# Idle-time products of a constant in the first stage of a fused state-space and channel-mix kernel

## What is computed

```python
mod = (silu(c) @ wmod).reshape(4, 6, 1, 512)
sa, ca, ga, sb, cb, gb = ...           # ga, gb pushed away from 0 to at least 0.25
h = layernorm(x) * (1 + ca) + sa
omega = clip(softplus(h @ W_omega.T + b_omega), 1e-4, 100); zeta = sigmoid(h @ W_zeta.T + b_zeta)
A = omega**2; S = 1 / (1 + 1e-4 * A); d = 1 - zeta; F = h @ W_B.T + b_B
# step: z' = d*(S*z - 0.01*A*S*y) + F_z ;  y' = d*(0.01*S*z + S*y) + F_y
x = x + ga * (states @ C.T + h @ D_mat.T)
h = layernorm(x) * (1 + cb) + sb
xr = mu_r*h + (1-mu_r)*h_prev;  xk = mu_k*h + (1-mu_k)*h_prev
x = x + gb * (sigmoid(xr @ W_r.T) * (relu(xk @ W_k.T)**2 @ W_v.T))
```

## Time and profile before

| | |
|---|---|
| median of three runs | 959.48 us (959.30 to 960.77) |
| the profiled execution | 959.10 us, of which the span is 957.3 us |
| TensorE busy | 932.2 us, 97% of the span |
| VectorE, ScalarE, GpSimd busy | 86%, 73%, 10% |
| mean granted clock of TensorE | 0.989 |
| the chain that ended last | 85% PE, 6% DVE, 6% ACT, 2% DMA |

### The profile page before, as it was taken

The page is one execution under the profiler, slowest core; times in us unless marked ns, Lnnn a source line. Parts: engine busy times, 40 slices in busy tenths (PEclk is TensorE's granted clock), DMA queues, the critical chain, the costliest instruction groups (busy, mean ns, idle before and its releaser), DMA issues.

```text
span 957.3 us, 14783 instructions
## 1 busy us (share of the span) xinstructions
PE 932.2 (97%) x5024; PEld 784.6 (82%) x5024; DVE 820.9 (86%) x2273; ACT 697.6 (73%) x1371; POOL 100.1 (10%) x117
## 2 busy tenths in 40 slices
PE   9998888999999999999999999999999999999998
PEld 3576776788888888888888888888888888888887
DVE  4898889898989989898997989899898989979664
ACT  4979886967777686777868777786877778766552
POOL 0000001020101102010110201011020102000000
PEclk9999979999999999999999999999999999999999
DMA  9810311120211312021121302112120211111001
GB/s 327 291 58 23 111 45 44 41 92 1 89 56 46 100 45 78 12 88 45 46 99 45 100 1 89 45 50 83 45 100 13 77 55 45 45 45 45 23 23 45
DMA packets 35435, 64.78 MB, mean 68 GB/s; under 512 B 3736, under 2 KB 4632, under 8 KB 35360
## 3 DMA queue, kind: packets, MB, share of 16 engines
q1 hardware_dynamic: 35360, 63.84, 19.7%
HBM read 47.02 MB, written 16.81 MB: 67 GB/s over the span
## 4 chain that ended last, share of the span: by engine, by line
PE 85%; DVE 6%; ACT 6%; DMA 2%; issue 1%; SPq 0%; ACTq 0%; DVEq 0%
PE ps_kr L340 34%; PE ps_cd L340 21%; PE ps_tv L340 17%; PE ps_pt L340 7%; PE ps_tv L381 3%; PE ps_pt L348 2%; ACT mix_full L762 1%; DMA stage_out<-in_wd 1%; PE ps_cd L388 1%; DVE mix_full L1017 1%; ACT x_in L628 1%; DMA x_in<-in_x 1%; PE ps_tv L401 0%; DVE ee L1131 0%; DVE tmp L1250 0%
## 5 line engine op out<-in xcount | busy, mean ns | idle before, releaser
L1017 DVE SCALAR_TENSOR_TENSOR mix_full<-ps_tv,cur_m,mix_full 128x256 f32<-128x256 f32 x256 | 117.8, 481 | 29.3 <-ACT mix_full L762 29.1
L784 ACT ACTIVATE kk<-ps_kr 128x512 f32<-128x512 f32 x64 | 38.1, 599 | 121.3 <-PE ps_kr L340 121.0
L762 ACT ACTIVATE mix_full<-ps_tv,cur_m 128x255 f32<-128x255 f32 x256 | 120.1, 573 | 7.5 <-PE ps_tv L381 7.5
L1529 POOL TENSOR_SCALAR var<-sq 128x2 f32<-128x2 f32 (+1 forms) x35 | 50.4, 1439 | 661.2 <-ACT square_out L610 661.2
L340 PE MATMUL ps_kr<-mix_k_hi,wk_hi 128*128 128x256 f32 x512 | 79.9, 278 | 4.6 <-issue 2.6
L340 PE MATMUL ps_kr<-mix_k_hi,wk_lo 128*128 128x256 f32 x512 | 79.2, 277 | 0.0
L340 PE MATMUL ps_kr<-mix_k_lo,wk_hi 128*128 128x256 f32 x512 | 79.2, 277 | 0.0
L340 PEld LDWEIGHTS ps_kr<-mix_k_hi,wk_hi 128*128 128x128 f32 x512 | 70.1, 188 | 7.9 <-issue 5.4
L340 PE MATMUL ps_kr<-wr_hi,mix_r_hi 128*128 128x512 f32 x248 | 68.7, 399 | 2.6 <-ACT kk L784 2.6
L340 PE MATMUL ps_cd<-wd_hi,h_hi 128*128 128x512 f32 x248 | 69.1, 401 | 0.0
L340 PEld LDWEIGHTS ps_kr<-mix_k_lo,wk_hi 128*128 128x128 f32 x512 | 68.1, 188 | 0.0
(11 more groups left out here) (236 smaller groups left out, 2265.1 us busy)
## 6 DMA issues: line engine op xcount, KB each, us to landing
x<-in_x SPq DMA_DIRECT2D x32, 512.0 KB, 3.7
out<-x SPq DMA_DIRECT2D x31, 512.0 KB, 2.8
x_in<-in_x SPq DMA_DIRECT2D x15, 1024.0 KB, 5.1
x<-in_wmod SPq DMA_DIRECT2D x3, 1024.0 KB, 7.4
mix_full<-in_wmod SPq DMA_DIRECT2D x2, 1024.0 KB, 9.3
x_in<-in_x SPq DMA_DIRECT2D x2, 512.0 KB, 5.3
stage_out<-in_wd SPq DMA_DIRECT2D x1, 1024.0 KB, 9.7
stage_mix<-in_wmod SPq DMA_DIRECT2D x1, 1024.0 KB, 11.0
```

The costliest lines, as they stand in the source:

```text
L762: mm = act.activation(mix[n][:, k, 1:UNIT], ps_tv[:, j, c * UNIT:(c + 1) * UNIT - 1], ACT.Identity, bias=cur_m[:, SHIFT + k:SHIFT + k + 1] ...
L784: act.activation(kk[:, i, :], ps_kr[:, i, :], ACT.Relu).then_inc(s_relu, 1)
L1017: dve.scalar_tensor_tensor(mix[n][:, k, :], ps_tv[:, j, c * UNIT:(c + 1) * UNIT], cur_m[:, alpha + k:alpha + k + 1], mix[n][:, k, :], ALU. ...
L1529: pool.tensor_scalar(var[:, :], sq[:, :], 1.0 / D, EPS, ALU.mult, ALU.add).then_inc(s_var, 1)
```

## The change

`keep_busy(bank, count)` issues `count` products of the constant, 128x512 each in bf16, into a bank of PSUM. The change calls it in three more places on TensorE, each behind a wait that tells that the bank isn't being read any more:

- stretch B: behind `v_product(1)`, before `states_part(2, ps_cd)`: 14 products into bank 0 of `ps_pt`, after `s_pev >= 3` (the projections of chunk 2 have been evicted);
- stretch C: behind `k_product(2)`, before `t2_blocks(3)`: 11 products into bank 0 of `ps_pt`, after `s_h` says that chunk 3 is evicted whole;
- stretch D: in `cd_product(4)`, between `h_part` and the wait for the states: 12 products into bank 0 of `ps_tv`, after `s_mix >= 32` (the mixes of unit 3 are done).

```diff
             def cd_product(u):
                 pe.wait_ge(s_gated, u * TPU)
                 h_part(u, ps_cd)
+                if u == 4:
+
+                    pe.wait_ge(s_mix, 4 * 2 * KC)
+                    keep_busy(ps_tv[:, 0, :], 12)
                 pe.wait_ge(s_xs_hi, u // 2 + 1)
                 pe.wait_ge(s_xs_lo, u // 2 + 1)
                 states_part(u, ps_cd)
@@
             r_product(1)
             projections(2)
             v_product(1)
+
+            pe.wait_ge(s_pev, 3)
+            keep_busy(ps_pt[:, 0, :], 14)
             pe.wait_ge(s_xs_hi, 2)
             pe.wait_ge(s_xs_lo, 2)
             states_part(2, ps_cd)
@@
             for u in range(2, NUNIT):
                 q = u // 2
                 k_product(u)
+                if u == 2:
+
+                    pe.wait_ge(s_h, h_done(3, 3))
+                    keep_busy(ps_pt[:, 0, :], 11)
                 if u + 1 < NUNIT:
                     transposed_mixes_in(u + 1)
```

## The result

| | before | changed |
|---|---|---|
| median of 20 runs each | 959.85 us (957.96 to 961.90) | 958.14 us (956.41 to 960.35) |
| ratio | | 0.9984, 95% interval 0.9978 to 0.9990 |
| the profiled execution | 959.10 us | 958.24 us, span 956.5 us |
| mean granted clock in it | 0.989 | 0.996 |

The change makes the kernel 0.16% faster, clear of zero and within the 0.2% that the forecast called no change. The forecast was 958.0 us, worked out from 959.48 us, the median of the first three runs of the kernel before.

A forecast was written before the change was run, and what follows sets the result against it. TensorE, at full clock from 174 us on, was taken as the bound; gains of 0.5 (B), 0.34 (C) and 0.64 us (D) sum to 1.48, giving 958.0 us, range 956.2 to 960.0 (8 in 10).

The forecast's parts named there:

- The bound: From 174.15 us to the end TensorE is busy 779.25 of 783.16 us, so arriving earlier there shows at the end.
- The price of the fillings: Each of the 37 added 128x512 products was to take 0.23 us of TensorE at the high clock.
- B: Before the states product of unit 2: a shorter low clock was to gain 0.5 us at the transposes of unit 2.
- open pause: Unfilled TensorE wait for x_in behind the states product of unit 2, 122 to 125 us: 3.0 us, clock falls after it.
- rival 1: The clock stays high everywhere: B is worth 1.86 us, the sum 2.84, time 956.6 us; chance 0.26.
- C: Before the transposes of unit 3: no low clock at 147; DVE's wait for ACT goes, gaining 0.34 us.
- D: Before the states of unit 4: v_product(2) at high clock gains 0.64 us, the rest becoming a wait for xn.
- the pause at D: TensorE's pause before the states of unit 4: 4.4 us, 2.8 us of it filled, 1.6 to 2.0 us left.
- rival 2: The clock falls at B and at D too: the sum is 0.84 us, time 958.6 us; chance 0.18.
- pauses of 2.60 us or more: On TensorE in the profiled execution, each was followed by a low clock of at least 3.41 us; none of 1.98 or less.
- stretch A: TensorE's pause from 75.27 to 77.87 us, 2.60 us, with the clock low from 78.58 for 3.41 us; left alone.
- rival 4: Slower: the products at C and D run at the low clock, 0.42 us each; time 962.4 us; chance 0.06.

The follow-up runs named there:

- second_pause: The changed kernel plus 12 products in the open pause behind the states product of unit 2; 957.93 us against 960.87 before, ratio 0.9972.
- d_only: The changed kernel without the products of stretches B and C; 959.27 us against 960.25 before, ratio 0.9993.
- c_long: The changed kernel with 22 products at stretch C instead of 11; 959.76 us against 960.87 before, ratio 0.9995.
- c_only: The changed kernel without the products of stretches B and D; 960.12 us against 960.25 before, ratio 0.9998.
- changed_again: The changed kernel without an edit, run again beside the last kernels; 959.05 us against 960.46 before, ratio 0.9982.
- b_and_c: The changed kernel without the products of stretch D; 959.50 us against 960.25 before, ratio 0.9991.
- second_pause_alone: The changed kernel with stretch B's 14 products taken out and 12 put into the open pause; 959.15 us against 960.87 before, ratio 0.9986.
- all_pauses: The changed kernel with the open pause, stretch A and the pause before k_product(1) filled too; 956.62 us against 960.46 before, ratio 0.9963.

## Why the prediction was right, and where it wasn't

- **The bound.** From 174 us on TensorE was to take over whatever it gained before. It did: the transposes of unit 4 are 1.19 us earlier, and those of the last batch, at 851.74 and 850.59 in the two traces, 1.15. Of this 0.3 us are lost in the last unit, at the full clock in both: its 48 products of `k_product` take 5.65 us (936.50 to 942.15) instead of 5.46 (937.66 to 943.12), and the 128x256 products at the very end are slower by the same 3 to 4%. What slows them isn't known.
- **The price of the fillings** was put at 0.23 us a product; it is 0.216. The covers were put at 1.0, 0.6 and 0.6 us or more; what was left is 1.17, 0.53 and 0.91 us.
- **B.** Forecast: a low stretch of 3.4 us behind the open pause, 0.5 us gained. Measured in the changed kernel's trace: low from 126.00 for 3.41 us, and 0.43 us. The open pause was put at 3.0 us and was 2.75. The open pause costs 1.43 us, by second_pause; rival 1 had put its worth at 1.36.
- **C.** Forecast 0.34 us; 0.45 in the changed kernel (22.29 to 21.84), 0.43 alone. The term was DVE's wait of 0.34 us for ACT at its first mix of unit 3 (150.65 in the earlier trace rows). It is gone, and the mix comes 0.42 us sooner behind the transposes (150.15 - 147.32 against 150.65 - 147.40):

```profile
150.15 0.48 DVE L1028 SCALAR_TENSOR_TENSOR mix_full<-ps_tv,cur_m,mix_full 128x256 f32<-128x256 f32 x1
```

- **D.** Forecast 0.64 us; 0.66 us, and the wait of about 1 us for `xn` of unit 4 is there with 0.95. That this normalisation hangs on the recurrence and not on `v_product(2)` can be read off: its second half begins 12.86 us behind the first states product in the earlier trace rows (182.55 - 169.69) and 12.85 us behind it now:

```profile
182.01 0.54 DVE L1055 TENSOR_SCALAR xn<-x,neg_mean,rstd 128x512 f32<-128x512 f32 x1
```

- **The sum** was 1.48 us; by sections it is 0.43 + 0.02 + 0.45 + 0.66 = 1.56. The medians of twenty differ by 1.71 us. The two profiled executions differ by 0.86 us, since the changed one was 0.37 us later before it came to B and lost the 0.3 us at the end.
- **A term that was mis-sized:** the pause at D was to grow by 1.06 us to 4.4. It grew to 3.53 and 3.56 in the kernels without the filling there. I had let TensorE pass from the transposes of unit 3 straight to the projections of chunk 4; at the high clock it waits 0.61 us for `h_lo` there. The pause left at D behind the filling was therefore 0.91 us and not 1.6 to 2.0, which made rival 2 less likely than I had it.
- **A step that was wrong:** that pauses of 2.60 us or more are followed by a low clock and those up to 1.98 us aren't. It came from four falls in one execution. The pause of stretch A, 2.58 to 2.60 us behind the same code, was followed by a fall in eight of the eleven traces that leave it open, the pause of 2.75 us at B in three of five; only the four of 4.1 to 4.5 us at B all had one. Pauses of 1.99 and 2.01 us at 92 were followed by a fall at 95 in d_only and c_long; those of 1.96 and 1.98 at the same place in two others were not, so the 1.98 us of the sum was no safe length either. 2.58 us at 76 had no fall behind it in c_only, 2.75 us none in c_long and changed_again, 3.53 us none in b_and_c. The Trainium skill (TensorE: Matmul & The Clock Gate, What's actually happening) says that the point of a change isn't tied to the start of the kernel and differs by run. The traces agree: the same code showed falls at 78 and 126 in one execution and at 78 and 95 in another. I had cited this under rival 2 and given it no weight in the sum. The pattern that I took for certain is one of several, and that the median came out as forecast is in part luck. It fits that this pattern, or one of the same cost, is the commonest: 13 of the 20 runs of the changed kernel lie between 957.6 and 958.3 us. The runs at 956.41 and, in changed_again, at 957.06, both with a mean clock of 0.998, fit rival 1; those above 959 us have the fall at 94 as their likely cause, which I had not on my list at all. For a single run both are argued from the traces of others, not shown.
- **Slower** (rival 4) didn't happen by itself. Made on purpose in second_pause_alone, products at the low clock cost 0.8 us at the next step of the chain.

## What to carry to other kernels

Products of a constant in a pause are worth what the clock would have cost behind the pause, on the chain that ends the stage, and no more: 8.0 us of filling gave 1.6 us. List all pauses ahead of and behind the one you fill, since a quicker engine comes to the next one sooner: here the two pauses that were left open (at 92 and at 123 us) cost more, some 1.4 us each when the clock fell, than any of the three that were filled gave. Judge falls of the clock from several executions, by the mean clock of each run, and never from one trace; and count the cover of a filling exactly, since at C every product beyond it went straight into the time.

## What the runs showed of the hardware

- A fall of the clock behind a pause of 2.0 to 3.6 us is a matter of the execution, as listed above. In 13 traces no low stretch was shorter than 3.41 us (those cut off by the end of the execution aside), and the longer ones were 6.83 and 10.24 us, in which TensorE stood still for 1.40 and 2.78 us.
- A tiny GpSimd operation, `var<-sq` of 128x2, took 0.52 or 0.53 us at one place in eleven traces and 3.00 us in two (second_pause and changed_again). It lies on the chain to the second normalisation and costs 1.0 us in the second section there. From the timelines of GpSimd and DVE, second_pause first and then all_pauses:

```profile
141.72 3.00 POOL L1541 TENSOR_SCALAR var<-sq 128x2 f32<-128x2 f32 x1 [13.56 <-ACT square_out L622]
144.25 0.42 DVE L1176 TENSOR_TENSOR tree<-tmp,f 128x256 f32<-128x256 f32 x1
144.80 0.70 POOL L1543 TENSOR_TENSOR rstd<-var,minus_half 128x2 f32<-128x2 f32 x1
```

```profile
141.95 0.52 POOL L1545 TENSOR_SCALAR var<-sq 128x2 f32<-128x2 f32 x1 [13.56 <-ACT square_out L626]
142.56 1.02 POOL L1547 TENSOR_TENSOR rstd<-var,minus_half 128x2 f32<-128x2 f32 x1
```

  It starts 0.22 us behind a 128x512 DVE operation in both, so that start doesn't explain it. The end does in part: the long one ends at 144.72, 0.05 us behind the last of a run of DVE operations that follow each other without a pause (144.25 and its 0.42 us). It is the same in changed_again (146.49 and 146.43) and in the kernel before, where the operation at 197.66 takes 3.65 us and ends 0.06 us behind such a run at 201.25. In all_pauses DVE is as busy and the operation gets through after 0.52 us. So by these rows the long ones wait for DVE to stand still; why some get through is open.
